# Eight-layer fp32 transformer on one core: values of two heads projected unturned in the first attention, keys copied ahead of the exponentials

## What is computed

```python
x = _rmsnorm(_layernorm(hidden), ln_weight)
h_q = (x @ w_q.T).reshape(b, lq, H, DH)
h_k = (key_value_states @ w_k.T).reshape(b, lk, H, DH)
h_v = (key_value_states @ w_v.T).reshape(b, lk, H, DH)
score = einsum('bqhd,bkhd->bhqk', h_q, h_k) + position_bias[None]
# masked keys out, softmax over k, rows without a live key to zero
out = einsum('bhqk,bkhd->bqhd', probs, h_v) @ w_out.T
```

## Time and profile before

| | us |
|---|---|
| median of 3 runs | 3165.69 |
| lowest, highest | 3163.64, 3179.11 |
| the profiled execution | 3167.79 |
| its span, first to last instruction | 3165.7 |
| TensorE busy | 2978.8 (94%) |
| VectorE, ScalarE, GpSimd busy | 1805.9, 1051.2, 1003.6 |
| mean granted TensorE clock | 0.982 |

### The profile page before, as it was taken

How to read it: one execution, slowest core, us unless ns; L and a number is a source line. 1 busy time by engine, 2 the same in 40 slices (tenths; PEclk the granted TensorE clock), 3 DMA queues, 4 the chain that set the end, 5 groups by cost and what they waited for, 6 DMA issues and landing times.

```text
span 3165.7 us, 46949 instructions
## 1 busy us (share of the span) xinstructions
PE 2978.8 (94%) x15712; PEld 2488.2 (79%) x15712; DVE 1805.9 (57%) x3657; ACT 1051.2 (33%) x3498; POOL 1003.6 (32%) x842
## 2 busy tenths in 40 slices
PE   4899999999998998989989999999989999999899
PEld 3788888888887875768877888888767888888687
DVE  7454444444454238878766666666674554454744
ACT  2222222222222216732234444444313333333332
POOL 3423334333322126533422322233213333332221
PEclk9999999999999999989999999999999999999899
DMA  3111111111111101101111100111011111110111
GB/s 103 43 36 36 42 42 42 42 42 42 34 42 47 40 20 42 33 27 34 45 30 31 34 25 25 33 33 33 24 34 37 34 36 42 37 33 20 44 41 50
DMA packets 69139, 119.71 MB, mean 38 GB/s; under 512 B 8745, under 2 KB 14249, under 8 KB 68641
## 3 DMA queue, kind: packets, MB, share of 16 engines
q1 hardware_dynamic: 69026, 118.26, 12.6%
HBM read 116.06 MB, written 2.10 MB: 37 GB/s over the span
## 4 chain that ended last, share of the span: by engine, by line
PE 82%; DVE 12%; ACT 3%; issue 3%; DMA 0%; DVEq 0%; POOL 0%; ACTq 0%; SPq 0%
PE proj L382 38%; PE outp L382 22%; PE heado L873 6%; PE score L844 4%; PE turn L864 2%; PE score L382 2%; PE turn L796 1%; DVE stats L431 1%; DVE x L1116 1%; PE outp L1741 1%; PE score L1326 1%; ACT tbuf L968 1%; DVE xnT L505 1%; ACT sq L956 1%; ACT acts L987 1%
## 5 line engine op out<-in xcount | busy, mean ns | idle before, releaser
L382 PE MATMUL outp<-w_out,acts 128*128 128x512 f32 x3288 | 849.6, 402 | 18.9 <-DVE x L1116 11.4
L382 PE MATMUL proj<-xnT,w_in 128*128 128x512 f32 x3288 | 783.6, 394 | 6.4 <-DVE xnT L505 2.6
L382 PEld LDWEIGHTS proj<-xnT,w_in 128*128 128x128 f32 x3288 | 614.9, 189 | 137.7 <-issue 6.0
L382 PEld LDWEIGHTS outp<-w_out,acts 128*128 128x128 f32 x3288 | 598.8, 190 | 145.5 <-DVE x L1116 16.3
L382 PE MATMUL proj<-ctxT,w_kv 128*128 128x512 f32 x2304 | 555.9, 398 | 19.2 <-ACT big L920 13.9
L382 PEld LDWEIGHTS proj<-ctxT,w_kv 128*128 128x128 f32 x2304 | 431.8, 190 | 125.2 <-ACT big L920 18.3
L645 POOL TENSOR_TENSOR w_out<-ring,consts 128x512 fp32r<-128x512 f32 x96 | 105.6, 1100 | 926.6 <-PE outp L382 926.6
L1116 DVE TENSOR_TENSOR x<-x,outp 128x512 f32<-128x512 f32 x384 | 262.2, 685 | 189.1 <-PE outp L382 187.4
L923 DVE COPY big<-proj 128x512 f32<-128x512 f32 x136 | 93.9, 690 | 386.0 <-PE proj L382 385.8
L645 POOL TENSOR_TENSOR w_kv<-ring,consts 128x512 fp32r<-128x512 f32 x96 | 100.6, 1047 | 428.5 <-DMA ring<-in_L_wk 427.2
L1140 DVE TENSOR_TENSOR acts<-heado,acts 128x512 fp32r<-128x512 f32 x192 | 132.8, 692 | 174.0 <-ACT acts L987 174.0
(11 more groups left out here) (246 smaller groups left out, 3956.7 us busy)
## 6 DMA issues: line engine op xcount, KB each, us to landing
ring<-in_L_wq SPq DMA_DIRECT2D x96, 256.0 KB, 2.7
ring<-in_L_wo SPq DMA_DIRECT2D x96, 256.0 KB, 2.7
ring<-in_F_in SPq DMA_DIRECT2D x52, 256.0 KB, 2.6
ring<-in_L_wk SPq DMA_DIRECT2D x48, 256.0 KB, 2.7
ring<-in_L_wv SPq DMA_DIRECT2D x48, 256.0 KB, 3.8
ring<-in_F_out SPq DMA_DIRECT2D x41, 256.0 KB, 2.7
x<-in_x SPq DMA_DIRECT2D x2, 1024.0 KB, 7.4
ring<-in_ctxT SPq DMA_DIRECT2D x8, 256.0 KB, 4.9
```

The costliest lines, as they stand in the source:

```text
L382: mm = pe.matmul(bank_ap, w_ap(a, c), rhs(b, c), start=first and c == 0 and n == 0, stop=last and c == chunks - 1 and n == len(PASSES) - 1)
```

## The change

1. The values of the first attention are projected unturned, two heads at a time. For each batch the context tile `ctxT[:, a, c, t]` (128 tokens) is stationary and 256 columns of weights (two heads) stream. Two batches fill one PSUM bank; four fills make the pair (`project_values`). The host lays out `L0_wv` so that each of two 256 KB tiles holds half of the inner dimension for both heads. Fills 0 and 2 are copied by ScalarE, 1 and 3 by VectorE, straight into `v_pair`, which takes the place of `vT` and `v` (`take_values_fill`).
2. `turn_values` and both its copies are gone from the first attention; its turns per group go from 16 to 8.
3. The order of projections changes. `needed` gives, in even heads, the keys of the head after next, the values of the pair (g, j), the query; in odd heads keys and query. The pair of heads 0 and 1 is projected ahead, in `pe_tail`. Tile order, projection numbers and waits follow; GpSimd waits for the values of the previous pair before it overwrites their weights.
4. ScalarE copies the first projection, the keys, before the exponentials of half 0 instead of after.
5. VectorE executes 32 waits on `consts_landed` (reached since the start) ahead of the third attention.

The core of the diff:

```diff
+DVE_ALIGN = 32
-        self.turns = 16 if self.own_kv else 12 if self.normed else 10
-        self.turns_first = 4 if self.normed else 2
+        self.turns = 8 if self.own_kv else 12 if self.normed else 10
+        self.turns_first = 0 if self.own_kv else 4 if self.normed else 2
...
-    OWN_FIRST = [("k", 0, 0), ("v", 0, 0), ("q", 0, 0), ("k", 0, 1), ("q", 0, 1)]
-    OWN_TILES = [("v", 0, 1), ("k", 0, 2), ("q", 0, 2), ("o", 0, 0), ("v", 0, 2), ("k", 0, 3), ("q", 0, 3), ("o", 0, 1),
-                 ("v", 0, 3), ("k", 1, 0), ("q", 1, 0), ("o", 0, 2), ("v", 1, 0), ("k", 1, 1), ("q", 1, 1), ("o", 0, 3)]
+    OWN_FIRST = [("k", 0, 0), ("v", 0, 0), ("v", 0, 1), ("q", 0, 0), ("k", 0, 1), ("q", 0, 1)]
+    OWN_TILES = [("k", 0, 2), ("q", 0, 2), ("o", 0, 0), ("k", 0, 3), ("q", 0, 3), ("o", 0, 1), ("v", 0, 2), ("v", 0, 3),
+                 ("k", 1, 0), ("q", 1, 0), ("o", 0, 2), ("k", 1, 1), ("q", 1, 1), ("v", 1, 0), ("v", 1, 1), ("o", 0, 3)]
...
+        v_pair = big[:, 2:4, :].rearrange("p a n -> p (a n)").rearrange("p (b h d) -> p b h d", b=B, h=2)
...
+                if A.own_kv and what == "v":
+                    if not (isinstance(g, int) and g == 0 and j < 2):
+                        m.wait(pool, ("pfull", 1), A.projection(*((g, 0) if j >= 2 else (g - 1, 2)), "v") + 2)
+                    split(g, j, "v", (w_kv, w_kv2)[j % 2], 1)
+                    return
...
-                value = [] if is_last_group(g) and j == GH - 1 else [(*h1, "v")]
-                return value + ([] if over else [(*h2, "k"), (*h2, "q")])
+                value = [] if j % 2 or isinstance(g, int) and g == 0 and j == 0 else [(g, j, "v")]
+                return value if over else [(*h2, "k"), *value, (*h2, "q")]
...
+        def project_values(pe, A, g, j):
+
+            m = A.events
+            n = A.projection(g, j, "v")
+            m.wait(pe, "split", A.tile(g, j + 1, "v") + 1)
+            for fill in range(4):
+                half = fill % 2
+                m.wait(pe, ("pfree", half), n + fill // 2)
+                for k in range(2):
+                    t = slice((2 * fill + k) * S, (2 * fill + k + 1) * S)
+                    mm = pe_matmuls(pe, proj[half][:, k * 2 * P:(k + 1) * 2 * P], lambda a, c: ctxT[:, a, c, t],
+                                    lambda b, c: (w_kv, w_kv2)[c // 2][:, 1, b, c % 2 * 2 * P:(c % 2 + 1) * 2 * P])
+                mm.then_inc(m["pfull", half], 1)
...
+                    if A.own_kv and j % 2 == 0 and half == 0:
+                        for i in range(2):
+                            m.wait(pe, ("pfree", i), A.projection(g, j, "v") + 2)
...
+        def take_values_fill(engine, on_act, A, g, j, fill):
+
+            m = A.events
+            half = fill % 2
+            m.wait(engine, ("pfull", half), A.projection(g, j, "v") + 1 + fill // 2)
+            dst = big[:, 2 + fill // 2, fill % 2 * HALF:(fill % 2 + 1) * HALF]
+            copy_projection(engine, on_act, dst, proj[half][:, :], None).then_inc(m["pfree", half], 1)
...
-                takes = [[], news[:1], news[1:]]
+                takes = [news[:1], [], news[1:]] if A.own_kv else [[], news[:1], news[1:]]
+                for new in takes[0]:
+                    take_projection(act, True, A, *new)
...
+            for _ in range(DVE_ALIGN):
+                dve.wait_ge(consts_landed, 32)
             dve.wait_ge(mask_landed, 32)
             attention_dve(dve, LA[2])
```

More of the change, by code:

```diff
@@ L162, in projection @@
         if self.own_kv:
-            if start and j == 0:
-                return "kvq".index(what)
-            return self.projections * g + (3 * j + "kqv".index(what))
+            if start and (j == 0 or j == 1 and what != "v"):
+                return {"k": (0, 4), "v": (1,), "q": (3, 5)}[what][j]
+            if start and (j, what) == (2, "k"):
+                return 6
+            if what == "v" and j >= 2 and isinstance(g, int) and g == NG - 1:
+                return self.projections * g + 10
+            return self.projections * g + {"k": (-2, 2, 4, 8), "q": (1, 3, 7, 9), "v": (5, 5, 11, 11)}[what][j]
         if start and j < 2 and what != "k":
@@ L174, in turn @@
         if self.own_kv:
-            order = ["T0", "T1", "V0", "V1"]
-            at = 4 * j
+            order = ["T0", "T1"]
+            at = 2 * j
         elif self.normed:
@@ L741, in new_values @@
         def new_values(A, g, j):
-            return A.new_kv((j + 1) % GH) and not (isinstance(g, int) and g == NG - 1 and j == GH - 1)
+            return not A.own_kv and A.new_kv((j + 1) % GH) and not (isinstance(g, int) and g == NG - 1 and j == GH - 1)
         def pending(A, g, j):
@@ L767, in project_head @@
             n = A.projection(g, j, what)
+            if A.own_kv and what == "v":
+                project_values(pe, A, g, j)
+                return
             w, slot, act = {"k": (w_kv, 0, ctxT), "v": (w_kv, 1, ctxT), "q": (w_in, j % 2, xnT)}[what]
-            if A.own_kv and what != "q" and j % 2:
+            if A.own_kv and what == "k" and j % 2:
                 w = w_kv2
@@ L872, in step @@
                     for b in range(BH):
-                        mm = pe.matmul(heado[:, b * P:(b + 1) * P], v[:, (half * BH + b) * S:(half * BH + b + 1) * S],
+                        n = half * BH + b
+                        mm = pe.matmul(heado[:, b * P:(b + 1) * P], v_pair[:, n, j % 2, :] if A.own_kv else v[:, n * S:(n + 1) * S],
                                        ptbuf[:, half, b * P:(b + 1) * P], start=True, stop=True)
@@ L901, in attention_pe @@
                 turn_for_sums(0, 0, "q", taken=(0, 0, "q"))
-            for half in range(2):
+            for half in range(2 if not A.own_kv else 0):
                 turn_values(-1, 3, half)
@@ L929, in take_projection @@
             half = 0 if on_act else 1
+            if A.own_kv and what == "v":
+                for fill in (half, half + 2):
+                    take_values_fill(engine, on_act, A, g, j, fill)
+                return
             m.wait(engine, ("pfull", half), A.projection(g, j, what) + 1)
@@ L1002, in attention_act @@
                 sum_squares(0, 0, "q")
-            take_values(act, True, A, -1, 3)
+            if not A.own_kv:
+                take_values(act, True, A, -1, 3)
             exps(0, 0, 0)
@@ L2275, in layout @@
     a["vecs"] = vecs
-    a["L0_wq"], a["L0_wk"], a["L0_wv"] = (tiles(i[f"L0_xattn_w_{n}"]) for n in "qkv")
+    a["L0_wq"], a["L0_wk"] = (tiles(i[f"L0_xattn_w_{n}"]) for n in "qk")
+    a["L0_wv"] = i["L0_xattn_w_v"].reshape(NH // 2, 2 * P, 2, 2, P).transpose(0, 2, 4, 3, 1).reshape(NH, P, D)
     a["L0_wo"] = i["L0_xattn_w_out"].T.reshape(NH, P, D)
```

5 lines of the change are left out of this document (3 added, 2 removed).

## The result

| | before | after |
|---|---|---|
| median | 3166.03 us (4 runs) | 3133.31 us (4 runs, 3130.43 to 3143.94) |
| ratio | | 0.9893, interval 0.9874 to 0.9912 |
| profiled execution, its span | 3167.79, 3165.7 us | 3132.72, 3130.9 us |

The changed kernel is 1.07% faster, 33 us in the medians and 34.8 in the spans. A second series on another chip gave 0.9897 (interval 0.9881 to 0.9912). The forecast was 28.1 us.

What follows compares the result with a forecast made beforehand. TensorE's stream, busy 94% of the span, was taken as the bound. +12.8 - 28.4 - 2.2 - 8.8 - 2.6 + 1.1 = -28.1 us from 3165.7 gave 3138 us, 0.9% faster; range 3115 to 3168 us.

Steps and rivals of the forecast that it cites:

- what is late next: First heads: VectorE's half of the keys, leaving 1.1 us of the 3.53 us wait in head (1,0), nothing in other early heads.
- Part 1: First attention's value projection: 1536 matmuls of 256 columns at 0.1233 us replace 768 of 512 at 0.230, +12.8 us.
- Part 3: First heads: ScalarE's early key copy removes five waits, 8.8 us, and 2.6 us of lower clock; free in the steady part.
- half-hidden: Rival on narrow matmuls: a straight line between widths gives 0.149 us each, 3177 us in all; 12 in 100.
- unhidden load: Rival on narrow matmuls: the stationary load isn't hidden, 0.218 us each, +145 us, 3283 us; 8 in 100, lesser degrees included.
- Part 2: First attention: 256 transposes of values go at 0.111 us each, -28.4 us, and 2.2 us of waits before them.
- It doesn't do what it says: Rival: VectorE's half of the keys sets the same date in all five places; -17.8, 3148 us; 12 in 100.
- the fifth wait (3.53): Head (1,0): TensorE idles 3.53 us for ScalarE's copy of the keys; 1.1 us of it was forecast to stay.
- Part 4: First attention's uneven heads, some 35 and 20 us: VectorE about 3 us late to scores, no TensorE wait; put at 0.
- Part 5: Start: two heads of values projected ahead, same idle, 72 narrow matmuls in 10.6 us; 0 beyond other terms, bounds -1 and +3.
- Part 6: Ahead of the third attention: VectorE's 32 waits cost 0, at most +5 us; the loop lies 8 instructions further on.
- the rival with VectorE's program: Third attention's loop, moved by 8, no longer fits and fetches instructions each turn: say +20 us, 3158 us; 8 in 100.

Runs made afterwards that it cites:

- the widths: The changed kernel plus 32 matmuls of each of 11 widths behind its last output product: 0.1197 us each at 256 columns, 0.1116 at 224.
- the doubled turns: The changed kernel with every turn of probabilities of the first attention done twice, 256 transposes more: 3160.37 us, ratio 0.9979.
- the early copy alone: The kernel before with only ScalarE's copy of a head's first projection moved ahead of the exponentials: 3154.34 us against 3168.0, ratio 0.9959.
- the version with the filled start: The changed kernel with VectorE's first key copy and value fills earlier at the start, next-layer preparation behind first copies: 3124.93 us; again 3123.51, ratio 0.9858.
- the 88 waits: The changed kernel with 88 instead of 32 waits of VectorE ahead of the third attention: one execution of 3141.07 us.
- the experiment with the late copy: The changed kernel with ScalarE's copy of the first projection back behind the exponentials of half 0: 3168.70 us against 3168.0, ratio 1.0002.

## Why the prediction was right, and where it wasn't

The forecast of 28.1 us was 4.6 us short of the medians (32.7) and 6.7 of the spans (34.8). What it says of TensorE's stream holds; the price of the narrow matmuls and what is late next were off in opposite ways, and a wait that no list shows was missing. That it came so near is in part luck.

**Part 1, the narrow matmuls.** The step with a mechanism was the right one: 0.1195 us in the kernel and 0.1197 by themselves, against 0.1233. The error is in the remainder: I took all 0.017 us above streaming from the 512-column row, and it is 0.013 at 256. With 0.1195, and 11.18 us for 48 wide ones (285.70 to 296.88, 0.233 each, where I had taken the mean with the query's; the other head of a pair took 11.43, with the short wait that belongs to Part 3), the term is 183.6 - 178.9 = +4.7 us instead of +12.8. This is the largest mis-sized term, 8 us. The rivals of a half-hidden and of an unhidden load are refuted by the row of 96 and by the widths. The rule that a load overlaps a matmul only at another row group (the Trainium skill, TensorE: Matmul & The Clock Gate, Part 3, "The mechanism") would give 0.218 us here; the measured 0.1195 decides against it for this stream. The same section also lets a load go ahead when it targets the "background weight buffer"; no row here shows which way the loads took.

**Part 2, the turns.** 0.109 to 0.111 us each by the doubled turns, and no turn of values left in the first attention: -28 us and the 2.2 of waits, as said.

**Part 3, the early copy.** The copied projection was named wrongly: in the kernel before `needed` begins with the values, so the five waits were for the copy of values, and in the changed one the keys come first. The size for the first heads was right (10.3 against 10.9 measured). What it says of the steady part, that later exponentials cost nothing there, came out as said. What it left out is what the early copy is worth there: 0.24 us in each pair already in the kernel before, 2.9 in all, which I had read as a stretch without gaps; and in the uneven order, with the copy in its old place, 1.50 us in each pair (54.97 against 53.47). I had priced the early copy in the old schedule alone. That the change held both parts saved the prediction, and that was luck: it has no term for it. "It doesn't do what it says" was wrong: no wait for ScalarE's copies of projections is left from 30 to 935 us, and VectorE's half took over 3.3 us in three places, not 8.8 in five.

**What is late next** was sized at 1.1 us at one place. That place has 0.83 us (at 191.84). The sentence that nothing is left in the other early heads failed: 1.91 and 0.58 us for VectorE's half in two heads before it, some 2 of lower clock, and 0.94 before the first scores. I had looked at the fifth wait (3.53) and left out what VectorE does at the end of each head of the first group, though Part 3's own copy stands behind it in VectorE's queue. A missing row of VectorE, not a wrong rule.

**Part 4, uneven heads.** 34 and 20 us, forecast 35 and 20, and no wait listed in the steady part. VectorE comes to the scores 4.3 us late, forecast 3. For the changed kernel 0 was right; but the lateness counted as harmless is what made the early copy necessary.

**Part 5, the start.** 5.20 us of idle time instead of 4.39, and the 72 matmuls took 10.70 us (52.35 to 63.05), forecast 10.6: at 0.1195 they would be 8.6, so the lower clock cost 2.1. Within the bounds.

**Part 6, the waits.** They cost nothing that shows, as said: VectorE idles 1.15 us for ScalarE at that point in both kernels. The loop lies where it lay, not 8 further on; and the rival with VectorE's program has a real mechanism, at a price of 11 us in the loop rather than 20. It did not come true because of the 32 waits. I had judged them by what they cost and not by what they put back.

**The sum with measured terms:** +4.7 - 28.2 - 2.2 (turns) - 11.4 (waits for ScalarE and lower clock) + 0.8 and 0.9 (start) + 3.3 and 1.5 (new waits in the first group, lower clock) + 0.6 (lower clock at the start, 2.1 against 1.5 before) + 0.8 (a new wait for `x` in the last head) - 1.0 (a wait of the first turn of probabilities that went) - 1.3 (ahead of the first projection) - 2.9 (the short waits of the steady pairs, as the early copy alone removed them) = -34.4 us, against 34.1 at the end of the first attention. The single terms are not known so well as this agreement looks: by them a steady pair should be 1.71 us shorter, and it is 1.61.

## What to carry to other kernels

A matmul may be made narrower for nothing down to the width at which its streaming time meets the load of its stationary tile, here between 224 and 256 columns; below it each costs the same 0.111 us, so measure that floor before splitting. Before calling a reordering on a side engine free, look at its slack in the schedule that the rest of the change makes, not in the old one; compare starts of the same work, since a wait of 0.2 us hides in overlapping durations; and list everything in that engine's queue ahead of the copy that the busy engine will want. When instructions are taken out ahead of a long loop of an engine, look afterwards for instruction packets inside the loop: the price of a shifted loop can be a third of the gain.

## What the runs showed of the hardware

**One stretch of TensorE ran wholly at the lower of its two clocks in some executions and mostly at the higher in others.** The 96 matmuls of 136 columns in the mixture stand behind 6.2 to 7.6 us of idle time and 16 transposes. They and the two instructions around them, in the changed kernel and in the first profile of the version with the filled start (columns as in the earlier trace rows):

```profile
2280.34:2292.07 11.73, 11.73 (x98) 11.73 (x97) 3.48 (x9) 0.72 (x2) 0.00 (x0) 0.91 0.01 1
```

```profile
2272.11:2292.64 20.53, 20.53 (x98) 20.53 (x97) 3.49 (x10) 0.73 (x2) 0.00 (x0) 0.50 0.00 1
```

The granted clock is 0.50, 1.2 GHz, for all of the 20.53 us, and the same work takes 8.8 us more; the profile with doubled turns has it too (20.53 us, behind 7.56 us of idle time, where the changed kernel had 7.55). The second profile of the version with the filled start has 11.71 us, so it belongs to the execution and not to the kernel. What decides it isn't shown. Single runs of the changed kernel, 3129.4 to 3135.7 us, with one of 3143.4 and one of 3143.9, fit two such cases; but the profiled ones among them all had the higher clock there, so for those two runs it is only argued. A look at the spans alone would have charged these 9 us to the edit; the starts of the same work before and behind the stretch do not.

**A stationary load of 128x128 adds nothing that shows under 256 columns.** Above streaming, 0.013 us are left at 256 columns as at 512. Rates per width are in the experiment; the floor of 0.111 us holds from 64 to 192 columns, to 0.001 us.

**VectorE waited for its own instructions in a loop,** 3.7 to 3.9 us per turn, when the loop lay 16 instructions lower in its program. With the 88 waits it stood still for 3.39 and 3.65 us in straight code; that this was for instructions isn't shown.

**An operation of VectorE can last until one of GpSimd's has ended:** 1.05 us instead of 0.16, both ending at 291.8, in the rows of the experiment with the late copy, and 0.79 in the kernel before (ends at 311.23 and 311.21). Not every pair does so: beside GpSimd's next operation in the kernel before (311.30 to 313.12) VectorE's three took their usual 0.68 and 0.69 us. TensorE has no listed wait for GpSimd there, and yet GpSimd's time seems to set in part when VectorE comes to the scores; that is read from the times, and no run moved it.
